# Layer 2's edge network: its edge values in three bf16 parts instead of one float32

## The reference

```
h = x[src] @ We1[:D] + x[dst] @ We1[D:] + be1        # one row for each edge
edge_new = relu(h) @ We2 + be2
agg = segment_sum(edge_new, dst)                     # edges are sorted by dst
x = layernorm(x + (x + mlp(concat[x, agg])))
```

## Time and profile before

| | |
|---|---|
| median of 3 runs | 6164.49 us (6153.3 to 6164.83) |
| the profiled execution | 6162.2 us, span 6160.4 us |
| TensorE matmul busy | 5555.2 us, 90% |
| VectorE busy | 4416.3 us, 72% |
| ScalarE busy | 2019.9 us, 33% |
| GpSimd busy | 1360.3 us, 22% |
| layer 2's edge network | from 3606.5 us (first gather) to 5137 us |

### The profile page before, as it was taken

One profiled execution on the slowest core, in us unless ns is written; L12 is line 12 of the kernel. 1 busy time (PEld: TensorE's weight loads), 2 busy tenths in 40 slices (PEclk: granted clock), 3 DMA queues, 4 the chain that ended last, 5 costly groups with the idle time before them and its releaser, 6 DMA issues. The chain is left out here.

```text
span 6160.4 us, 165256 instructions
## 1 busy us (share of the span) xinstructions
PE 5555.2 (90%) x58225; PEld 4851.5 (79%) x58310; DVE 4416.3 (72%) x7547; ACT 2019.9 (33%) x4615; POOL 1360.3 (22%) x1304
## 2 busy tenths in 40 slices
PE   3999988999999999999996879999999998699986
PEld 2888876888888888888885569999999996456655
DVE  7999942777777777777774457777777774388874
ACT  0000033333433434433432322222222221266651
POOL 1444445333333333333332310000000000200000
PEclk9999999999999999999998989999999997899988
DMA  6444412222222222222220123333333330100000
GB/s 122 149 158 149 158 56 79 88 88 85 85 85 85 88 86 82 88 88 81 88 80 18 37 98 117 121 118 118 115 123 117 119 115 34 57 5 0 0 1 22
DMA packets 206210, 523.66 MB, mean 85 GB/s; under 512 B 33555, under 2 KB 85398, under 8 KB 199318
## 3 DMA queue, kind: packets, MB, share of 16 engines
q1 hardware_dynamic: 195936, 518.35, 24.7%
q10 hardware_dynamic: 10179, 4.02, 0.3%
HBM read 485.12 MB, written 37.19 MB: 85 GB/s over the span
## 5 line engine op out<-in xcount | busy, mean ns | idle before, releaser
L1279 PE MATMUL ps<-kv_table,stage 128*128 128x256 bf16 x7644 | 1252.5, 273 | 29.4 <-DVE stage L1135 27.3
L1251 POOL TENSOR_TENSOR message<-message 128x512 f32<-128x512 f32 (+1 forms) x676 | 724.4, 1072 | 1468.9 <-ACT message L1213 1468.9
L1294 PE MATMUL ps<-message,slot_hot 128*128 128x136 f32 x5200 | 779.2, 292 | 121.2 <-POOL message L1251 102.6
L1667 PE MATMUL ps<-a_table,stage 128*128 128x128 bf16 x7644 | 843.7, 219 | 31.3 <-DVE stage L1550 31.3
L1670 PE MATMUL ps<-window,stage 128*128 128x128 bf16 x7800 | 861.3, 219 | 0.0
L1282 PE MATMUL ps<-window,stage 128*128 128x128 bf16 x7800 | 860.6, 219 | 0.0
L1294 PEld LDWEIGHTS ps<-message,slot_hot 128*128 128x128 f32 x5200 | 649.2, 190 | 212.1 <-POOL message L1251 167.8
L1142 DVE TENSOR_TENSOR slot_hot<-iota,slots 128x512 f32<-128x512 f32 (+1 forms) x676 | 452.5, 669 | 452.7 <-PE ps L1294 452.7
L1569 DVE TENSOR_TENSOR slot_hot<-iota,slots 128x512 f32<-128x512 f32 (+1 forms) x676 | 454.1, 672 | 416.5 <-PE ps L1682 401.4
L1620 ACT ACTIVATE edge<-ps 128x512 f32<-128x512 f32 x624 | 373.4, 598 | 1105.9 <-PE ps L1682 1068.8
L1279 PEld LDWEIGHTS ps<-kv_table,stage 128*128 128x128 bf16 x7644 | 669.1, 98 | 71.5 <-issue 27.9
(11 more groups left out here) (335 smaller groups left out, 7606.3 us busy)
## 6 DMA issues: line engine op xcount, KB each, us to landing
stage<-lists SPq DMA_DIRECT2D x312, 768.0 KB, 4.1
edges<-in_edge_attr SPq DMA_DIRECT2D x52, 1984.0 KB, 7.6
stage<-lists SPq DMA_DIRECT2D x104, 896.0 KB, 5.4
window<-qkv_rows SPq DMA_DIRECT2D x52, 288.0 KB, 4.7
...
```

What stands on the lines that cost most here:

```text
L1251: pool.tensor_tensor(values, values, message[n % 2][:, 0:nt, D:D + HEADS].unsqueeze(3) .broadcast_to([P, nt, HEADS, HEAD]), ALU.mult).then ...
L1279: nc.tensor.matmul(kv_ps[n % 2][:, i, :], from_src, kv_table[:, tile, q, :], start=(q == 0), stop=(q == 2))
L1294: last = nc.tensor.matmul(ps[:, 6 + d, 0:D + HEADS], slot_hot[n % 2][:, i, :], message[n % 2][:, i, :], start=(tile == 0), stop=(tile == S ...
L1667: nc.tensor.matmul(edge_ps[n % 2][:, i, :], from_src, a_table[:, tile, q, :], start=(q == 0), stop=False)
```

## The change

The edge values are kept in three bf16 parts, as the tables are. `high` is the relu, rounded to bf16, by ScalarE. `rest` is relu minus high in float32, by VectorE, straight from PSUM. The middle part is the upper half of rest's float32 words, read in place: a bf16 view of rest that takes every second element (`middle`). The low part is rest minus middle, by GpSimd, which had no work in this stage. The scatter has two bf16 matmuls for each tile: one of 258 columns (high, low, two count columns) and one of 128 (middle). The slot one-hots become bf16, in layer 3's form, with the tile number innermost. At a group's end four float32 matmuls instead of two join the three sums.

Two of VectorE's tasks change. The own one-hots move to ScalarE in two passes, relu(1 - |lane - number|). The degrees are summed as bf16 halves into a running sum for the whole stage, and reduced once at its end. Buffers become four or five instead of two, TensorE gathers three batches ahead, and the hots are built two batches earlier. Some early weights share their space with the running sum, and five counters of passed waits become one. A list's buffer is now free when both VectorE and ScalarE have used it.

The new parts of the diff, with what they replace:

```diff
+        DEPTH = 5
+        REUSE = 4
+        BUFFER = [n % 4 for n in range(NB2 - 6)] + [4, 0, 1, 2, 3, 4]
+        DIRECT = 2 * D + EXTRA
+        SUMS = DIRECT + D
...
-            slot_hot = [sb(f"slot_hot2_{i}", [P, 4, P], scope=scope) for i in range(2)]
-            edge = [sb(f"edge{i}", [P, 4, D + EXTRA], scope=scope) for i in range(2)]
-            edge_last = [sb(f"edge_last{d}", [P, 2, D + EXTRA], scope=scope) for d in range(2)]
-            group_sum = [sb(f"group_sum2_{d}", [P, D + EXTRA], scope=scope) for d in range(2)]
-            degrees = [sb(f"degrees{i}", [P, UT], scope=scope) for i in range(2)]
+            slot_hot = [sb(f"slot_hot2_{i}", [P, P, 4], BF16, scope=scope) for i in range(DEPTH)]
+            number1_by4 = sb("number1_by4_2", [P, P, 4], BF16, scope=scope)
+            parts = [sb(f"parts{i}", [P, 4, DIRECT], BF16, scope=scope) for i in range(DEPTH)]
+            parts_last = sb("parts_last", [P, 2, DIRECT], BF16, scope=scope)
+            rest = [sb(f"rest2_{i}", [P, 4, D], scope=scope) for i in range(DEPTH)]
+            group_sum = sb("group_sum2", [P, SUMS], scope=scope)
+            degree_sum = early[:, 0:NB * P // 4].bitcast(BF16).rearrange("p (t s) -> p t s", s=P // 2)
+            degrees = dis[:, 0:NB]
...
+            edge_ps = [ps[:, i, :].rearrange("p (t f) -> p t f", f=D) for i in range(DEPTH)]
+            GROUP_ACC = ps[:, 5, 0:P]
+            GROUP_COUNTS = ps[0:EXTRA, 5, P:2 * P]
+
+            middle = [part[:, :, :].rearrange("p t f -> p (t f)").bitcast(BF16).rearrange("p (t f h) -> p t f h", f=D, h=2)
+                      [:, :, :, 1] for part in rest]
+
+            def parts_of(n):
+                b = n % BATCHES
+                return parts[BUFFER[n]] if b < BATCHES - 1 else parts_last
...
+                                    sp.wait_ge(own2, pair * 8 + d * 4 + u + 1)
...
+                @block.gpsimd
+                def _(pool):
+                    total = rounds(pool)
+                    pool.sem_inc(low2, REUSE)
+                    with loop(pool, 0, total) as pair:
+                        for n in range(NB2):
+                            s, nt = pair * NB2 + n, len(batch_tiles(n % BATCHES))
+                            pool.wait_ge(rest2, s + REUSE + 1)
+                            pool.sem_inc(pool_waited, 1)
+                            pool.tensor_tensor(parts_of(n)[:, 0:nt, D:2 * D], rest[BUFFER[n]][:, 0:nt, :],
+                                               middle[BUFFER[n]][:, 0:nt, :], ALU.subtract).then_inc(low2, 1)
...
-                        dve.tensor_scalar(hots[u % 2][0][:, 0:n], lists_b[u % 2][:, 0, 0:n], lane1[:, :], None, ALU.is_equal)
+                        dve.wait_ge(degree2, 2 * k + 14)
                         dve.tensor_scalar(hots[u % 2][1][:, 0:n], lists_b[u % 2][:, 1, 0:n], lane1[:, :], None,
                                           ALU.is_equal).then_inc(hots2, 1)
...
-                        dve.tensor_reduce(degrees[u % 2][:, 0:nt],
-                                          hots[u % 2][1][:, 0:nt * P].rearrange("p (t s) -> p t s", s=P), AX.X,
-                                          ALU.add).then_inc(degree2, 1)
-                        dve.wait_ge(degree2, k * 2 + 5)
-                        dve.tensor_tensor(deg[:, first_tile:end], deg[:, first_tile:end], degrees[u % 2][:, 0:nt],
-                                          ALU.add).then_inc(degree2, 1)
-
-                    def batch(pair, g, n):
+                        folded = hots[u % 2][1][:, 0:(end - first_tile) * P].rearrange("p (t h s) -> p t h s", h=2, s=P // 2)
+                        for h in range(2):
+                            dve.wait_ge(degree2, 2 * k + h + 16)
+                            dve.tensor_tensor(degree_sum[:, first_tile:end, :], degree_sum[:, first_tile:end, :],
+                                              folded[:, :, h, :], ALU.add).then_inc(degree2, 1)
+
+                    def slots_of(pair, g, n):
                         b, s = n % BATCHES, pair * NB2 + n
-                        nt = len(batch_tiles(b))
                         dve.wait_ge(scattered2, s + 1)
-                        dve.tensor_tensor(slot_hot[n % 2][:, 0:nt, :], over_chunks(iota1[:, :], nt),
-                                          over_columns(slots[:, ds(g, 1), 0, 4 * b:4 * b + nt]
-                                                       .rearrange("p s t -> p (s t)"), P),
+                        dve.tensor_tensor(slot_hot[BUFFER[n]][:, :, :], number1_by4[:, :, :],
+                                          slots[:, ds(g, 1), 0, 4 * b:4 * b + 4].broadcast_to([P, P, 4]),
                                           ALU.is_equal).then_inc(slot_hot2, 1)
+                    def rest_of(pair, n):
+                        s, nt = pair * NB2 + n, len(batch_tiles(n % BATCHES))
+                        dve.wait_ge(high2, s + 1)
+                        dve.wait_ge(scattered2, s + 1)
+                        dve.scalar_tensor_tensor(rest[BUFFER[n]][:, 0:nt, :], edge_ps[BUFFER[n]][:, 0:nt, :], 0.0,
+                                                 parts_of(n)[:, 0:nt, 0:D], ALU.max, ALU.subtract).then_inc(rest2, 1)
...
-                            batch(pair, g + d, n)
-                            if b in (0, 3, 6):
-                                unit_hots(pair, d, b // 3 + 1)
-                            if b == 9 and d == 0:
-                                unit_hots(pair, 1, 0)
-                            if b == 9 and d == 1 and ahead:
-                                unit_hots(pair + 1, 0, 0)
-                            if b in (1, 4, 7, 10):
+                            if n + 1 < NB2 or ahead:
+                                rest_of(pair + (n + 1) // NB2, (n + 1) % NB2)
+                            slots_of(pair, g + d, n)
+                            following = (pair, 1) if d == 0 else (pair + 1, 0)
+                            if b in (0, 3, 6, 9):
                                 unit_degrees(pair, d, b // 3)
-                            if n == 3 and behind:
+                            if b in (1, 4):
+                                unit_hots(pair, d, b // 3 + 2)
+                            if b in (7, 10) and (d == 0 or ahead):
+                                unit_hots(*following, b // 3 - 2)
+                            if n == 5 and behind:
...
+                        dve.wait_ge(degree2, first * 16 + 16 * PAIRS + 16)
+                        dve.tensor_reduce(degrees[:, :], degree_sum[:, :, :], AX.X, ALU.add).then_inc(flushed2, PAIRS)
+                        dve.wait_ge(flushed2, first * 3 + 2 * PAIRS + 1)
+                        dve.tensor_tensor(deg[:, 0:NB], deg[:, 0:NB], degrees[:, :], ALU.add).then_inc(flushed2, PAIRS)
...
+                        act.activation(parts_of(n)[:, 0:nt, 0:D], edge_ps[BUFFER[n]][:, 0:nt, :], ACT.Relu).then_inc(high2, 1)
...
+                    def own_apart(pair, d, u):
+                        n, k = (unit_tiles(u)[1] - unit_tiles(u)[0]) * P, pair * 8 + d * 4 + u
+                        behind = d * BATCHES + (UNITS[u - 2][1] if u >= 2 else UNITS[u + 2][1] - BATCHES)
+                        act.wait_ge(lists_in2[u % 2], pair * 64 + d * 32 + u // 2 * 16 + 16)
+                        act.wait_ge(gathered2, pair * NB2 + behind + GATHERED)
+                        act.activation(hots[u % 2][0][:, 0:n], lists_b[u % 2][:, 0, 0:n], ACT.Abs, bias=lane1[:, :],
+                                       scale=-1.0).then_inc(apart2, 1)
+
+                    def own_hot(pair, d, u):
+                        n, k = (unit_tiles(u)[1] - unit_tiles(u)[0]) * P, pair * 8 + d * 4 + u
+                        act.wait_ge(apart2, k + 1)
+                        act.activation(hots[u % 2][0][:, 0:n], hots[u % 2][0][:, 0:n], ACT.Relu, bias=ones[:, 0:1],
+                                       scale=-1.0).then_inc(own2, 1)
...
-                    def body(pair, behind):
+                        act.wait_ge(scattered2, pair * NB2 + d * BATCHES + BATCHES + REUSE)
+                        act.wait_ge(added2, j + 2 + 2 * DEPTH + 3)
+                        act.wait_ge(group_ps2, j + 1)
+                        act.activation(group_sum[:, :], ps[:, 6 + d, 0:SUMS], ACT.Copy).then_inc(group_sb2, 1)
+
+                    def body(pair, behind, ahead):
                         for n in range(NB2):
-                            relu(pair, n)
-                            if n == 1 and behind:
+                            d, b = n // BATCHES, n % BATCHES
+                            following = (pair, 1) if d == 0 else (pair + 1, 0)
+                            if n + 1 < NB2 or ahead:
+                                high(pair + (n + 1) // NB2, (n + 1) % NB2)
+                            if b in (1, 4):
+                                own_apart(pair, d, b // 3 + 2)
+                            if b in (2, 5):
+                                own_hot(pair, d, b // 3 + 2)
+                            if b in (7, 10) and (d == 0 or ahead):
```

(27 more changed lines are left out.)

128 lines of the change are left out of this document (68 added, 60 removed).

## The result

The changed kernel takes 6012.48 us (median of 4 runs, 6009.98 to 6023.82), the kernel before 6158.9 beside it (4 runs, 6150.59 to 6164.83). The ratio is 0.9773, with a 95% interval of 0.976 to 0.9787. It is faster by 146 us. The forecast was 6097, a gain of 67 us, with a range down to 6015. So the sign was right, the gain was more than twice the forecast, and the time lies 2.5 us under the range. 6015 is the number of rival 1, in which TensorE stays the bound.

A forecast was written before the change was run, and what follows sets the result against it. TensorE bounds the edge-network stage before, VectorE with GpSimd after: (27.8 - 29.2) x 52 = -73 us, +7 at the stage's ends, -66 in all, from 6162.2 or 6164.5 to 6097 us; range 6015 to 6210.

The forecast's parts named there:

- rival 1: Edge-network stage: TensorE stays the bound, GpSimd's operation being 1.0 us or fitting VectorE's gaps; 6015 or 6036 us; chance 0.24.
- TensorE after the change: Edge-network stage: four-tile scatter 0.68 us instead of 0.96, turn 0.45 dearer; TensorE alone 26.2 us a group, saving 157 us.
- ScalarE: Edge-network stage: with two passes over each unit's own one-hots, ScalarE has 20.1 us a group, under TensorE's 26.2.
- The pair VectorE and GpSimd: Edge-network stage: the two wait for each other at shared ports and become the bound, at 27.8 us a group.
- D = 1.155: GpSimd's low-part subtraction for each batch: 1.155 us, taken from a row with a bf16 second operand and 512 elements.
- the formula: Pace of VectorE with GpSimd in a group: 13 D + 12.8 us, D being the time of GpSimd's subtraction.
- a degree step: VectorE's step with two degree additions, between slot one-hots, four in a group: D + 1.85 us.
- a one-hot step: VectorE's step with a one-hot, between slot one-hots, four in a group: D + 1.27 us.
- The 0.6 taken off for the short batch: Sum of VectorE's 13 steps in a group: 0.6 us less because one batch has only two tiles.
- signs of being right: Edge-network stage: TensorE idle behind GpSimd's parts, VectorE's additions and one-hots well over 0.56 and 0.62 us, 128-column products at 59 ns.
- Ends of the stage: Start and end of the edge-network stage: +7 us, between 4 and 10, for ScalarE passes, wider turn, last chain and reduction.
- Rivals 2 and 3: Edge-network stage: GpSimd's strided reading slower, 6333 us at 1.5 us, chance 0.22; strided weights stall TensorE's scatter, 6195 us, 0.04.

The follow-up runs named there:

- the fourth experiment: Changed kernel without the middle part's matmul for 36 of a group's 50 tiles, and with the low part computed for half its columns: 5912.2 us, 0.9611.
- the first experiment: Changed kernel with GpSimd subtracting the packed high part instead of the strided middle part: 6049.44 us, 0.9814.
- the third experiment: Changed kernel with the scatter's matmul on the middle part left out for 36 of a group's 50 tiles: 6002.95 us, 0.9757.

## Why the prediction was wrong

**TensorE after the change: right.** Scatter of four tiles 0.68 (measured 0.68), strided products 59 ns (60), turn dearer by 0.45, a group 26.2 (26.27), worth 157 us (52 times the steady 3.01 is 156.5; 151 between first and last turn). The 22 ns more for a 128-column product, an estimate from the 81 ns of the Trainium skill (TensorE: Matmul & The Clock Gate, Back-to-back issue gap), do not show: leaving out 36 products in the fourth experiment saved 2.0 us, 55 ns each.

**ScalarE: right.** Its passes take 1.57 and 1.78 us, where I had 1.45 and 1.66, but a group has 883.96 / 45.5 = 19.4 us of work in all, under the 20.1 forecast. It holds nobody up but for the 0.4 us a group in which VectorE waits.

**The pair VectorE and GpSimd: the mechanism right, its size wrong, and with it the bound.** This is the step that failed: "I take D = 1.155, the row with the bf16 operand". That row's second operand is packed. The new operation reads every second bf16, and takes 1.053; with a packed one it would take 1.14 (the first experiment). In 13 steps this is 13 x 0.10 = 1.3 us a group, 69 us in all. The rest of the formula was too high too: with D = 1.053 it gives 26.5, where the third experiment shows 25.7, and at 1.14 it gives 27.6 against 26.7. Some 0.2 of that is only the mean over all turns against a steady group, which takes 25.90 in the third experiment. The other 0.6 is the sum of small excesses: a degree step has 2.90 by the formula and 2.83 in that trace, a one-hot step 2.32 and 2.25, a plain one 1.20 and 1.18, and a group has thirteen. The 0.6 taken off for the short batch was right.

With 25.7 the pair falls behind TensorE, which the prediction had at 26.2. So rival 1 happened, for the reason that it named first: a shorter GpSimd operation. The shorter operation alone did not decide it: by the formula the pair would still stand at 26.5, above TensorE, and the two errors were needed together. The sign came out right since TensorE's part was right. Of the prediction's signs of being right, the stretched one-hots and additions appeared and still did not mean that the pair was the bound; TensorE's idle time did, and it was absent. I gave rival 1 a chance of 0.24. Since both numbers lay within 0.4 to 1.6 us of each other by either of the two rows, that was too little, and a range that ended at this rival's exact time left no room below it.

**Ends of the stage: too small by half.** +7 forecast, between 4 and 10. From first gather to last turn the stage holds all 52 groups. It became 151.0 - 1.9 = 149.1 us shorter, where 52 steady groups give 156.5, so 7.4 went elsewhere; 5.2 of that is the pause where TensorE leaves its loop (31.6 - 26.4), which the prediction did not have. After the last turn it takes 6.9 more, of which the one reduction is 3.40. Together that is 14.3 and outside the 4 to 10. The profiled execution made up for it with the 8.0 us by which its stage began earlier, so it is in part luck that the time comes within 2.5 us of rival 1's 6015.

**Rivals 2 and 3: excluded.** The stride makes GpSimd faster, and the strided weights cost next to nothing (60 ns for a product where the packed gather has 55.5).

**What the chances missed.** The prediction held GpSimd's help for given and asked only for its price. With the low part on VectorE a group is only 0.18 us longer. The part of the change that counts, beside the bf16 products, is the move of the own one-hots (90 us).
